# One body for two neighbouring time chunks: joint projections, norms and inverse, convolution taps from an SBUF copy, decay from rows of cumulative sums

## The chip, the cores and the metric

The kernel runs on one NeuronCore of one Trainium2 chip. The metric is the device time of one launch in microseconds (us). The engines are TensorE (PE in the profile, its weight loads PEld), VectorE (DVE), ScalarE (ACT), GpSimd (POOL) and SyncE, whose queue (SPq) issues the DMAs.

## The reference, cut to what matters

```python
# x (8, 1024, 128); 16 heads, key width 64, value width 128, 4 taps; then x + layernorm(attn(layernorm(x)))
q = l2(silu(conv4(x @ Wq.T)));  k = l2(silu(conv4(x @ Wk.T)));  v = silu(conv4(x @ Wv.T))
alpha = exp(-exp(A_log) * softplus(x @ Wa.T + dt_bias));  beta = 2 * sigmoid(x @ Wb.T)
def step(S, q_t, k_t, v_t, a_t, b_t):
    kS = k_t @ S
    S = a_t * (S - b_t * outer(k_t, kS)) + outer(k_t, v_t)
    return S, S.T @ q_t
o = rms_norm(o);  y = o @ Wo.T
# then x = x + layernorm(y), and a small feed-forward layer (token shift, three 128x128 products) with its own residual
```

All of it is float32.

## The kernel before

The recurrence is run in chunks of C = 64 tokens. A **step** is one chunk (of 16) of one pair of heads (of 8) for all 8 sequences: `STEPS` = 128 steps, in order, since the state `S` passes from chunk to chunk. The two heads of a pair lie on partitions 0 to 63 and 64 to 127. Most products are therefore 64x64 or 64x128, four of them side by side on the quadrants of the PE array; `CLASSES` are the sequences 0 to 3 and 4 to 7, which use different quadrants.

What a step does, by the names of its functions:

- `pe_proj` j = 0 to 3 (k, q, v of head 0, v of head 1): two matmuls of 4 x 67 columns each into PSUM banks 0 and 1. All four projections use these two banks. `act_tap0` multiplies the first tap out of PSUM into `cv`, `dve_conv` adds three more (L852), reading the projection from PSUM and `cv` from SBUF, 512 elements per partition each. Then a Silu.
- Norms: `pe_nk`, `pe_nq`, `pe_ms` sum squares over partitions with a moving operand of one column.
- Decay: `pool_lm` masks the log decay into `Lm` (two instructions, L967), `pe_dec` (L513) sums it up with triangular matrices, `act_exp` takes the exponential, `pool_dmn` and `pool_dmp` scale and mask it. The reset at the start of each pair of heads is a log decay of -1e4 (`RESET`).
- Products `pe_gram_k`, `pe_gram_p`, `pe_ktr`, `pe_ks`, `pe_vtr`; `dve_n` times `exN` gives `Nd`, `pool_nm` masks it to `NM`.
- The inverse of the 64x64 triangular matrix: the diagonal 16x16 blocks go through DRAM (`scrN`) into a layout with 64 blocks on 64 partitions, `pool_elim` (13 small instructions) and `dve_sub` (4 instructions of 512 elements) invert them, they go back through DRAM (`scrZ`, `scrX`), and two rounds of `pe_y`, `pe_z` with copies `act_y`, `act_x`, `dve_z0`, `act_z1` build the rest in `Z`.
- The recurrence: `pe_ks` (k times S), `dve_r`, `pe_u`, `act_u`, `pe_ds`, `pe_o`, `dve_s` (new S), `pool_sg` (S times decay); then `act_oc`, `act_osq`, `pe_ms`, `pe_wo` (L706), `act_yr` (8 scaled copies), `pool_acc` (L1016).

The work is software-pipelined by hand: one body holds the end of step l, the middle of l + 1 and the front of l + 2. The order on every engine is written out in `pe_body`, `act_body`, `dve_body`, `pool_body` and `sp_body`, and `program` runs three bodies before and three after a hardware loop of 124 bodies. Each engine does its list strictly in order, and the waits between them are on semaphores.

```python
with eng.Fori(1, STEPS - 3) as i:
    body(eng, i, i + 1, i + 2)
```

Of the kernel before, what the change touches and what calls it, by code (L numbers as in the profile page):

```python
# [18 lines left out]
P = 128  # L19
# [20 lines left out]
RESET = -1.0e4  # L40
# [6 lines left out]
K_N = K_XI + 272  # L47


def constants():  # L50

    c = np.zeros((P, K_N), np.float32)
    i = np.arange(P)
    same = (i[:, None] // C) == (i[None, :] // C)
    r, t = (i % C)[:, None], (i % C)[None, :]
    c[:, K_ID:K_ID + P] = np.eye(P)
    c[:, K_LE:K_LE + P] = same & (r <= t)
    c[:, K_GT:K_GT + P] = same & (r > t)
    c[:, K_BD:K_BD + P] = same
# [4 lines left out]
    c[:, K_XI:K_XI + 256:17] = 1.0  # L64
    return c


class Signal:
# [12 lines left out]
def build(nc, x, wtab, wo, wab, hcol, cst, wf, mu, out):  # L81
    with ExitStack() as ctx:
# [75 lines left out]
        bd_zero = sig("bd_zero")  # L158
# [23 lines left out]
        with nc.Block() as block:  # L182
# [13 lines left out]
            def _(pool):  # L196
# [18 lines left out]
            def _(dve):
# [64 lines left out]
            def _(act):  # L280
                act.wait_ge(zeroed.sem, 6)
# [67 lines left out]

        wkq_in = sig("wkq_in", 16)  # L350
# [15 lines left out]
        silu_q = sig("silu_q")
        silu_v = sig("silu_v", 2)
# [18 lines left out]
        x_in = sig("x_in", 64)  # L386
        v_tr = sig("v_tr")
        v_ok = sig("v_ok")
        k_tr = sig("k_tr")
        kt_ok = sig("kt_ok")  # L390
        pe_go = sig("pe_go")
        sp_go = sig("sp_go")
        y_mm = sig("y_mm", 2)
        y_ok = sig("y_ok", 2)
        z_mm = sig("z_mm", 2)
        z_ok = sig("z_ok", 2)
        x_mm = sig("x_mm")
        x_ok = sig("x_ok")
        ks_mm = sig("ks_mm")
        os_mm = sig("os_mm")  # L400
        o_mm = sig("o_mm")
        ds_mm = sig("ds_mm")
        sg_ok = sig("sg_ok", 2)
        n2_ok = sig("n2_ok")
        r2_ok = sig("r2_ok")
        rv_ln = sig("rv_ln")
        rv_ok = sig("rv_ok")
        bn_ok = sig("bn_ok")
        cr_ok = sig("cr_ok")
        nqs_ok = sig("nqs_ok")  # L410
        xi_ok = sig("xi_ok")
        xb_ok = sig("xb_ok")
        r0_ok = sig("r0_ok")
        r1_ok = sig("r1_ok")
        u0_mm = sig("u0_mm")
        u1_mm = sig("u1_mm")
        u0_ok = sig("u0_ok")
        u1_ok = sig("u1_ok")
        s0_ok = sig("s0_ok")
        s1_ok = sig("s1_ok")  # L420
        osq_ok = sig("osq_ok")
        oc_ok = sig("oc_ok")
        ms_mm = sig("ms_mm")
        ro_in = sig("ro_in")
        ro_ln = sig("ro_ln")
        ro_ok = sig("ro_ok")
        wo_mm = sig("wo_mm")
        yr_ok = sig("yr_ok")
        acc_ok = sig("acc_ok", 2)

        tabP3 = tabP[:].rearrange("p (n k) -> p n k", k=24)
        tabR3 = tabR[:].rearrange("p (n k) -> p n k", k=16)
        cv4 = cv[:].rearrange("p (i b t) -> p i b t", i=4, b=NB)
        v3 = lambda t, i: t[:, i * 512:(i + 1) * 512].rearrange("p (b t) -> p b t", b=NB)
        pj = bank(0, 2).rearrange("p (b t) -> p b t", b=NB)
        half = lambda t, g: t[:, g * 512:(g + 1) * 512]
        sq_kt, sq_qt = half(sq, 0), half(sq, 1)
        exN, exP = half(ex, 0), half(ex, 1)
        CLASSES = (range(0, 4), range(4, 8))
        r0r1, u_mms, u_oks, s_oks = (r0_ok, r1_ok), (u0_mm, u1_mm), (u0_ok, u1_ok), (s0_ok, s1_ok)  # L440
        osq = BD["KB"]
        yt = (half(BD["X"], 1), half(BD["Y"], 1))
        n2, r2, rv, bn, cr, nqs, ro = (sc[:, 8 * k:8 * k + 8] for k in range(7))
        row = lambda t: t.rearrange("p (o k) -> p o k", o=1)
        acc3 = accT[:].rearrange("p (c k) -> p c k", k=512)

        PB = {"dec": 4, "nk": 2, "gk": 2, "nq": 4, "gp": 2, "ktr": 4, "vtr": 4, "y0": 4, "z0": 4, "x": 2, "y1": 4, "z1": 6, "ks": 6, "u": 2, "o": 2, "ds": 6, "ms": 2, "wo": 6}
# [6 lines left out]
        def first(n):  # L454
            return isinstance(n, int) and n == 0
# [9 lines left out]
        def blk64(t, b, a):  # L465

            return t[a:a + 64, b * C:(b + 1) * C]
# [9 lines left out]
        def pair(bk, o=0):  # L477

            return bank(bk, 2).rearrange("p (g n) -> p g n", g=2)[:, :, o:o + 4 * C]

        def tiny(bk):

            return bank(bk, 2).rearrange("p (g n) -> p g n", g=2)[:, :, 0:4]
# [5 lines left out]
        def sv_out(h):  # L489

            a = sv[:].rearrange("p (b h t) -> p b h t", b=NB, h=2)[:, :, h, :]
            (ps_, pn), (bs, _), (ts, tn) = a.ap
            return bass.AP(a.tensor, a.offset, [(ps_, pn), (4 * bs + (1 - 2 * h) * C, 2), (bs, 4), (ts, tn)])


        def pe_proj(pe, n, j):
            w_in = (wkq_in, wv_in)[j // 2]
            pe.wait_ge(w_in.sem, w_in.at(n))
# [7 lines left out]
        def pe_dec(pe, n):  # L506
# [626 lines left out]
        def sp_body(sp, l, m, n):  # L1133
            if l is not None:
                sp_x_in(sp, l)
# [501 lines left out]
```

## Time and profile before

| | |
|---|---|
| time, median of 3 runs | 3735.81 us (3723.3, 3735.81, 3737.05) |
| span of the profiled execution | 3725.1 us |
| busy share: PE, PEld, DVE, ACT, POOL | 88%, 74%, 70%, 72%, 62% |
| matmul records | 77978 |
| mean granted TensorE clock | 0.922 of full speed |
| DMA, all queues | 226.12 MB, 61 GB/s over the span |

The profiled execution has its span as its own time; the median of the runs lies 10.7 us above it. Busy is the time in which an engine executes an instruction. The clock is given in parts of full speed, 2.4 GHz; it has two levels, 1.2 and 2.4 GHz.

### The profile page before, as it was taken

The numbers are of one execution on the slowest core, as the hardware profiler recorded it, in microseconds if no ns is written. First come the engines' busy times: TensorE is split into PE (matmuls) and PEld (weight loads), VectorE is DVE, ScalarE is ACT, GpSimd is POOL, SyncE is SP. The second block draws the span as 40 slices with busy tenths as digits, with TensorE's granted clock in tenths as the row PEclk, the third lists the DMA queues.
The fourth block names the chain that finished last, engine by engine and source line by source line (L and its number), as shares of the span: only waits on it lengthen the run. The fifth ranks groups of instructions, "written<-read, shape, count | busy, mean of one in ns | idle before, by whom it ended". The sixth has DMA issues, their size and how long they took to land. (4 is left out here: it accounts for less than half of the span.)

```text
span 3725.1 us, 195058 instructions
## 1 busy us (share of the span) xinstructions
PE 3292.6 (88%) x77978; PEld 2742.6 (74%) x77978; DVE 2605.8 (70%) x5465; ACT 2677.6 (72%) x5548; POOL 2301.4 (62%) x3558
## 2 busy tenths in 40 slices
PE   5699999999999999999999999999999999999775
PEld 4577777777777777777777777777777777777643
DVE  6677777777777777777777777777777777777453
ACT  2577777777777777777777777777777777777553
POOL 2456666666666666666666666666666666666345
PEclk9789999999999999999999999999999999999777
DMA  2223223232323232323323232323233232323111
GB/s 59 52 61 64 62 62 67 57 67 56 69 56 70 58 66 58 66 59 64 64 60 64 60 67 57 71 57 67 61 63 64 60 65 59 65 59 70 42 34 46
DMA packets 911057, 226.12 MB, mean 61 GB/s; under 512 B 820128, under 2 KB 894112, under 8 KB 911008
## 3 DMA queue, kind: packets, MB, share of 16 engines
q1 hardware_dynamic: 910848, 224.91, 28.8%
q8 instruction: 33, 0.54, 0.1%
q0 software_dynamic: 160, 0.53, 0.0%
q14 instruction: 16, 0.13, 0.0%
HBM read 169.73 MB, written 55.58 MB: 60 GB/s over the span
## 5 line engine op out<-in xcount | busy, mean ns | idle before, releaser
L852 DVE SCALAR_TENSOR_TENSOR cv<-ps,w_kq,cv 128x512 f32<-128x512 f32 x768 | 575.5, 749 | 417.1 <-ACT cv L719 403.5
L852 DVE SCALAR_TENSOR_TENSOR cv<-ps,w_v,cv 128x512 f32<-128x512 f32 x768 | 575.4, 749 | 153.0 <-ACT cv L719 134.9
L1016 POOL TENSOR_TENSOR accT<-accT,X 128x512 f32 (+1 forms) x128 | 163.3, 1276 | 530.2 <-ACT Y L817 530.2
L502 PE MATMUL ps<-xnT,w_kq 128*128 (+1 forms) x1024 | 325.7, 442 | 74.6 <-DVE cv L852 69.0
L502 PE MATMUL ps<-xnT,w_v 128*128 (+1 forms) x1024 | 335.2, 453 | 15.2 <-DVE cv L852 15.0
L1007 POOL TENSOR_TENSOR Sg<-S,tabR 128x512 f32<-128x512 f32 x256 | 333.8, 1323 | 0.0
L976 POOL TENSOR_TENSOR sc<-tabP,sc 128x8 f32<-128x8 f32 x128 | 26.3, 206 | 497.5 <-DVE sc L867 497.5
L765 ACT ACTIVATE Vt<-ps,sc 128x128 f32<-128x128 f32 x1024 | 278.8, 384 | 54.8 <-PE ps L571 54.8
L706 PE MATMUL ps<-wo_s,oo 128*128 128x128 f32 x2048 | 305.6, 309 | 1.2 <-issue 1.2
L967 POOL TENSOR_TENSOR Lm<-k_all,tabP 128x512 f32<-128x512 f32 x256 | 277.2, 1102 | 30.5 <-POOLq L182 30.5
L706 PEld LDWEIGHTS ps<-wo_s,oo 128*128 128x128 f32 x2048 | 280.8, 220 | 14.5 <-issue 1.7
L952 DVE SCALAR_TENSOR_TENSOR Rr<-ps,sc,Vt 128x128 f32<-128x128 f32 x1024 | 288.2, 344 | 1.3
L696 PEld LDWEIGHTS ps<-k_all,KB 128*128 128x128 f32 x2048 | 240.6, 193 | 58.7 <-issue 58.7
L637 PEld LDWEIGHTS ps<-Rr,Z 64*64 64x64 f32 x4096 | 238.1, 141 | 54.5 <-issue 54.5
L502 PEld LDWEIGHTS ps<-xnT,w_kq 128*128 128x128 f32 x1024 | 184.1, 200 | 126.0 <-issue 93.2
L637 PE MATMUL ps<-Rr,Z 64*64 64x128 f32 x4096 | 269.1, 284 | 1.9 <-issue 1.9
L696 PE MATMUL ps<-k_all,KB 128*128 128x1 f32 x2048 | 248.3, 251 | 5.9 <-ACT KB L802 2.1
L585 PEld LDWEIGHTS ps<-Z,NM 64*64 64x64 f32 x8192 | 187.4, 166 | 78.6 <-issue 78.6
L808 ACT ACTIVATE oo<-ps 128x1024 f32<-128x1024 f32 x128 | 131.2, 1025 | 154.3 <-PE ps L653 154.3
L585 PE MATMUL ps<-Z,NM 64*64 64x64 f32 x8192 | 213.2, 255 | 29.2 <-DVE Z L941 28.1
L653 PE MATMUL ps<-PT,U 64*64 64x64 f32 x8192 | 216.7, 221 | 23.8 <-PE ps L650 22.8
L719 ACT ACTIVATE cv<-ps,w_kq 128x512 f32<-128x512 f32 x256 | 174.3, 681 | 74.8 <-PE ps L502 74.7
(197 smaller groups left out, 8542.9 us busy)
## 6 DMA issues: line engine op xcount, KB each, us to landing
ex<-scrG SPq DMA_DIRECT2D x256, 128.0 KB, 2.9
scrN<-Nd SPq DMA_DIRECT2D x256, 128.0 KB, 2.6
Z<-scrZ SPq DMA_DIRECT2D x256, 128.0 KB, 3.2
X<-scrX SPq DMA_DIRECT2D x512, 64.0 KB
w_kq<-wtab SPq DMA_DIRECT2D x128, 132.0 KB, 2.2
w_v<-wtab SPq DMA_DIRECT2D x128, 132.0 KB, 2.5
wo_s<-wo SPq DMA_DIRECT2D x128, 128.0 KB, 2.8
NS<-scrN SPq DMA_DIRECT2D x128, 64.0 KB, 2.6
```

The lines of the kernel that those rows point to most:

```text
L502: last = nc.tensor.matmul(pj[:, 4 * g:4 * g + 4, 0:CW], w[:, (j % 2) * P:(j % 2 + 1) * P], xnT3[:, 4 * g:4 * g + 4, bass.ds((n % NC) * C, ...
L585: last = nc.tensor.matmul(ps[place(cls, a), col64(PB["y1" if l else "y0"], cls, i)], blk64(BD["NM"], b, a), blk64(BD["Z"], b, a), start=Tr ...
L637: last = nc.tensor.matmul(ps[a:z, col128(PB["u"], g, i)], blk64(BD["Z"], b, a), unit(Rr, b)[a:z], start=True, stop=True)
L653: last = nc.tensor.matmul(o_cols(h ^ cls, b, d), U[a:z, b * P + d:b * P + d + 64], blk64(BD["PT"], b, a), start=False, stop=(b == NB - 1))
L696: last = nc.tensor.matmul(ps[:, (PB["ms"] + h) * 512 + i:(PB["ms"] + h) * 512 + i + 1], osq[:, h * 512 + i * P:h * 512 + (i + 1) * P], kc( ...
L706: last = nc.tensor.matmul(ps[:, col128(PB["wo"], h, i)], oo[:, h * 512 + i * P:h * 512 + (i + 1) * P], wo_s[:, h * D:(h + 1) * D], start=T ...
L719: nc.scalar.activation(cv4[:, j], pj[:, :, 0:C], ACT.Copy, scale=tap(j, 0)).then_inc(tap0[j].sem, 1)
L765: last = nc.scalar.activation(unit(Vt, b), unit(ps, 4 * PB["vtr"] + b), ACT.Copy, scale=rv[:, b:b + 1])
L852: nc.vector.scalar_tensor_tensor(cv4[:, j], pj[:, :, k:k + C], tap(j, k), cv4[:, j], ALU.mult, ALU.add).then_inc(conv[j].sem, 1)
L952: last = nc.vector.scalar_tensor_tensor(unit(Rr, b), ps[:, col128(PB["ks"], g, i)], cr[:, b:b + 1], unit(Vt, b), ALU.mult, ALU.add)
L967: last = nc.gpsimd.tensor_tensor(v3(Lm, i), over(kc(o, C), NB, C), tabP3[:, bass.ds(n, 1), 0:8].rearrange("p o b -> p b o").to_broadcast([ ...
L1007: nc.gpsimd.tensor_tensor(half(Sg, g).rearrange("p (b v) -> p b v", b=4), half(S, g).rearrange("p (b v) -> p b v", b=4), gam, ALU.mult).th ...
```

## The change

Two neighbouring chunks of the same pair of heads, A and B (128 tokens), become one **pair**: `PAIRS` = 64 of them. A body now holds pair p0 (front), p1 (inverse and recurrence, first A, then B), p2 (rest of B, output) and p3 (last accumulations).

- Projections: one matmul of 512 columns for four sequences, without the 3 halo columns. `act_raw` copies the product from PSUM to `raw` in SBUF; `pool_tail` carries the last 3 columns over from the pair before. All four taps read `raw`: `act_tap0` and `dve_conv` now work on 1024 elements per partition with both inputs in SBUF.
- Norms: `nk`, `nq`, `ms` use 64 columns of ones in place of 1, on quadrants (`ms`: halves of columns); the small vectors hold both chunks.
- Decay: the cumulative sums are made once, in the prologue, and their rows stored in DRAM (`scrE`, and `scrG` their exponentials). Per pair, `sp_gr` broadcasts a row to 64 partitions, `pool_diff` subtracts the column, `act_abs` and `act_exp` give exp(-|difference|). `pool_lm`, `pe_dec` and `pool_nm` go. The reset is now zeros in the tables.
- Inverse: elimination and substitution run once per pair on 128 partitions. `Y` and `X` are single buffers for A and B in turn.
- `act_yr` (ScalarE) becomes `dve_yr` (VectorE, one instruction of 512 per half). `bn` and `cr` go from POOL to DVE. `sp_kc` copies B's keys to `kB` by DMA, so that `sk` is free for the next pair.
- The lists of all five engines are new. The loop has 58 bodies; 6 bodies stand before it and 4 after it.

```diff
-        def pe_proj(pe, n, j):
+        def pe_proj(pe, p, j):
...
             for g in range(2):
-                last = nc.tensor.matmul(pj[:, 4 * g:4 * g + 4, 0:CW], w[:, (j % 2) * P:(j % 2 + 1) * P],
-                                        xnT3[:, 4 * g:4 * g + 4, bass.ds((n % NC) * C, CW)], start=True, stop=True)
+                last = nc.tensor.matmul(bank(PB["P" + "kqvw"[j]] + g), w[:, (j % 2) * P:(j % 2 + 1) * P],
+                                        xnV[:, 4 * g:4 * g + 4, bass.ds((p % 8) * P, P)], start=True, stop=True)
...
+        def act_raw(act, p, j):
+            act.wait_ge(proj[j].sem, proj[j].at(p))
+            act.wait_ge(tail[j].sem, tail[j].at(p))
+            nc.scalar.activation(raw3[j][:, :, HALO:HALO + P], b3(bank(PB["P" + "kqvw"[j]], 2)), ACT.Copy).then_inc(raw_ok[j].sem, 1)
...
-                nc.vector.scalar_tensor_tensor(cv4[:, j], pj[:, :, k:k + C], tap(j, k), cv4[:, j],
-                                               ALU.mult, ALU.add).then_inc(conv[j].sem, 1)
+            nc.vector.scalar_tensor_tensor(cv3[j], raw3[j][:, :, k:k + P], tap(j, k), cv3[j],
+                                           ALU.mult, ALU.add).then_inc(conv[j].sem, 1)
...
+        def pe_ms(pe, p, s):
...
+            for i in range(4):
+                for h in range(2):
+                    for e, (c, d) in enumerate(HALF):
+                        o = h * 512 + (2 * i + e) * C
+                        last = nc.tensor.matmul(ps[c:d, col64(PB["ms"][s], h, i)], osq[:, o:o + C], kc(K_ONE, C), start=True, stop=True)
...
+        def act_abs(act, p):
+            act.wait_ge(diff_ok.sem, diff_ok.at(p))
+            nc.scalar.activation(E[:], E[:], ACT.Abs).then_inc(abs_ok.sem, 1)
...
+        def dve_yr(dve, p, s, h):
+            dve.wait_ge(wo_mm[h][s].sem, wo_mm[h][s].at(p))
+            dve.wait_ge(rt_ok.sem, rt_ok.at(p + 1))
...
+            nc.vector.tensor_tensor(half(yt, h).rearrange("p (i d) -> p i d", i=4),
+                                    bank(PB["wo"][s] + h).rearrange("p (i d) -> p i d", i=4), f, ALU.mult).then_inc(yr_ok[h][s].sem, 1)
...
+        def pool_tail(pool, p, j):
...
+            nc.gpsimd.tensor_tensor(raw3[j][:, :, 0:HALO], raw3[j][:, :, P:P + HALO],
+                                    tails[:, bass.ds(p, 1)].rearrange("p (o u) -> p o u", u=1).to_broadcast([P, NB, HALO]),
+                                    ALU.mult).then_inc(tail[j].sem, 1)
...
+        def sp_gr(sp, p):
+            if not first(p):
+                sp.wait_ge(pt_ok[B].sem, pt_ok[B].at(p - 1))
...
+                sp.dma_start(E[a:z], scrE[h, bass.ds(p, 1), :].to_broadcast([C, 1024])).then_inc(gr_in.sem, 16)
...
+            for i in range(6):
+                body(eng, *at(i))
+            with eng.Fori(2, PAIRS - 4) as j:
+                body(eng, j + 4, j + 3, j + 2, j + 1, j)
+            for i in range(PAIRS, PAIRS + 4):
+                body(eng, *at(i))
```

The new lists of the loop body, in order (0, 1, 2, 3 stand for the pairs p0 to p3):

```
PE:   proj 0k, 0q; ms 2B; ds 2B; ktr 1B; wo 2A; vtr 1A; proj 0v1; ks 1A; nq 1; y0 1A; proj 0v0; z0 1A; gk 0A; nk 0; x 1A; y1 1A;
      wo 2B (half); z1 1A; y0 1B; wo 2B (half); u 1A (half); z0 1B; u 1A (half); vtr 1B (half); y1 1B; vtr 1B (half); gk 0B; ds 1A;
      o1 1A; x 1B; ktr 0A; o2 1A; ks 1B; z1 1B; ms 1A; gp 0A; u 1B; o1 1B; gp 0B; o2 1B
DVE:  p 1B; sub 1 (4); ro_in 2B; conv 0k.1; s 2B; k 1B; yr 2A; conv 0k.2; cr 1; conv 0k.3, 0q.1; r 1A; nqs 1; r 1A; z0 1A; n2 0;
      conv 0q.2, 0q.3; yr 2B; r2 0; conv 0v0.1; bn 0; yr 2B; z0 1B; conv 0v0.2; n 0A, 0B; s 1A; k 0A; conv 0v0.3; r 1B; ro_in 1A;
      conv 0v1.1; p 0A; conv 0v1.2, 0v1.3
ACT:  raw 0k; tap0 0k; raw 0q; xb 1; table; ln 1; tap0 0q; root 1; oc 2B; v 1A; raw 0v1; table; silu_k 0; y0 1A; sq_k 0; raw 0v0;
      tap0 0v0; x 1A; y1 1A; abs 0; z1 1A; y0 1B; table; exp 0; u 1A; y1 1B; v 1B; table; silu_q 0; x 1B; osq 1A; z1 1B; tap0 0v1;
      u 1B; oc 1A; silu_v0 0; osq 1B; silu_v1 0
POOL: tail 0k; sg 2B; xi 1; sq_q 1; elim 1 (13); acc 3B; tail 0v0, 0q; acc 3B; sg 2B; tail 0v1; acc 2A; sg 1A; diff 0; qg 1; acc 2A;
      sg 1A; eb 0A, 0B; ep 0
SP:   wkq 0; gram 1A, 1B; gram_in 1; kc 1; xr 1; gr 0; wo 2; wv 0; z_out 1; x_out 1; z_in 1; x_in 1A, 1B
```

## Rows read from the trace of the kernel before

**Rows 1.** The page's busy times: busy us, share of the span, instructions.

```profile
PE 3292.6 (88%) x77978; PEld 2742.6 (74%) x77978; DVE 2605.8 (70%) x5465; ACT 2677.6 (72%) x5548; POOL 2301.4 (62%) x3558
```

**Rows 2.** Windows: from:to, length, busy us of PE, PEld, DVE, ACT, POOL, clock, DMA share.

```profile
1000.00:1500.00 500.00, 458.52 (x11400) 386.54 (x11400) 363.48 (x704) 380.65 (x799) 326.40 (x514) 0.94 0.30 62
...
1546.00:1547.00 1.00, 1.00 (x30) 0.88 (x23) 0.72 (x2) 1.00 (x1) 1.00 (x2) 0.50 0.45 101
```

**Rows 3.** Timeline of PE: start, length, line, tiles, count, [idle before it and releaser].

```profile
1502.53 1.17 PE L502 MATMUL ps<-xnT,w_kq 128*128 x4 [0.50 <-DVE cv L852]
...
1528.93 1.17 PE L502 MATMUL ps<-xnT,w_kq 128*128 x4 [0.50 <-DVE cv L852]
1530.03 1.96 PE L637 MATMUL ps<-Rr,Z 64*64 64x128 f32 x32
...
1537.36 0.69 PE L564 MATMUL ps<-k_all,sl 64*64 64x64 f32 x32
...
1539.83 1.07 PE L513 MATMUL ps<-Lm,k_all 64*64 64x256 f32 x16
1540.94 1.92 PE L696 MATMUL ps<-k_all,KB 128*128 128x1 f32 x16
1543.21 0.64 PE L523 MATMUL ps<-k_all,sq 64*64 64x1 f32 x32 [0.35 <-DVE sc L881]
...
1553.11 1.06 PE L533 MATMUL ps<-k_all,sq 64*128 64x1 f32 x16 [0.33 <-ACT Y L780]
```

**Rows 4.** Groups by form, 1000 to 2000 us: busy us, mean ns, idle before.

```profile
L852 DVE SCALAR_TENSOR_TENSOR cv<-ps,w_kq,cv 128x512 f32<-128x512 f32 x228 | 170.9, 750 | 122.1 <-ACT cv L719 118.1
...
L967 POOL TENSOR_TENSOR Lm<-k_all,tabP 128x512 f32<-128x512 f32 x76 | 83.8, 1123 | 0.0
...
L1260 ACT ACT_TABLE_LOAD x38 | 48.8, 1283 | 0.7
...
L960 DVE TENSOR_TENSOR S<-ps,Sg 128x512 f32<-128x512 f32 x76 | 48.7, 682 | 6.7 <-PE ps L653 4.6 <-POOL Sg L1007 1.8
...
L1022 POOL TENSOR_TENSOR NM<-Nd,k_all 128x512 f32<-128x512 f32 x38 | 48.4, 1273 | 0.0
...
L817 ACT ACTIVATE Y<-ps,sc 128x128 f32<-128x128 f32 x148 | 42.9, 397 | 0.0
...
L928 DVE TENSOR_TENSOR tmpS<-XT,tmpW 64x512 f32<-64x512 f32 x38 | 40.6, 1068 | 1.3
...
L808 ACT ACTIVATE oo<-ps 128x1024 f32<-128x1024 f32 x38 | 38.9, 1025 | 43.6 <-PE ps L653 43.6
...
L921 DVE TENSOR_TENSOR tmpS<-NS,XT 64x512 f32<-64x512 f32 x38 | 33.2, 874 | 0.0
```

**Rows 5.** Groups by form with 1024 elements: a vector sum, a ScalarE pass.

```profile
L256 DVE TENSOR_TENSOR U<-U,S 128x1024 f32<-128x1024 f32 x1 | 1.2, 1226 | 4.0 <-ACT Rr L301 4.0
...
L1553 ACT ACTIVATE U<-U 128x1024 f32<-128x1024 f32 x8 | 8.5, 1057 | 0.3
```

**Rows 6.** Instructions of one line: ns min/median/max, whole span, then 1000 to 2000 us.

```profile
L921 DVE TENSOR_TENSOR tmpS<-NS,XT x128: 673/828/5560, 124.7 to 3481.0; 64x512 f32<-64x512 f32 x128
...
L1007 POOL TENSOR_TENSOR Sg<-S,tabR x76: 1031/1482/1772, 1005.8 to 1983.0; 128x512 f32<-128x512 f32 x76
```

**Rows 7.** Timeline of DVE in the first bodies.

```profile
124.74 3.59 DVE L921 TENSOR_TENSOR tmpS<-NS,XT 64x512 f32<-64x512 f32 x1
```

**Rows 8.** Timeline of POOL in the same stretch.

```profile
123.52 2.04 POOL L967 TENSOR_TENSOR Lm<-k_all,tabP 128x512 f32<-128x512 f32 x2
125.53 1.26 POOL L1029 TENSOR_TENSOR QG<-sl,ex 128x512 f32<-128x512 f32 x1
126.75 1.03 POOL L990 TENSOR_TENSOR sq<-sl 128x512 f32<-128x512 f32 x1
```

**Rows 9.** Timeline of PE behind the loop's end.

```profile
3457.50 0.46 PE L653 MATMUL ps<-PT,U 64*64 64x64 f32 x15 [0.93 <-issue]
...
3469.88 3.35 PE L706 MATMUL ps<-wo_s,oo 128*128 128x128 f32 x14 [0.89 <-issue]
```

More of the change, by code:

```diff
@@ new lines, in pe_ms, with pe_wo @@
+            last.then_inc(ms_mm[s].sem, 1)
+        def pe_wo(pe, p, s, h):
+            pe.wait_ge(wo_in.sem, wo_in.at(p))
+            pe.wait_ge(oc_ok[s].sem, oc_ok[s].at(p))
+            pe.sem_inc(pe_go.sem, 1)
+            for i in range(4):
+                last = nc.tensor.matmul(ps[:, col128(PB["wo"][s], h, i)], oo[:, h * 512 + i * P:h * 512 + (i + 1) * P],
+                                        wo_s[:, h * D:(h + 1) * D], start=True, stop=True)
+            last.then_inc(wo_mm[h][s].sem, 1)
@@ new lines, in act_ln, with act_ln_out @@
+        def act_ln(act, p):
+            act.wait_ge(n2_ok.sem, n2_ok.at(p))
+            if not first(p):
+                act.wait_ge(ro_in[B].sem, ro_in[B].at(p - 1))
+            act_ln_out(act, p)
+            nc.scalar.activation(sc[:, 32:64], sc[:, 0:32], ACT.Ln).then_inc(ln_ok.sem, 1)
+        def act_ln_out(act, p):
+            if not first(p):
+                for g in range(2):
+                    act.wait_ge(v_ok[g][B].sem, v_ok[g][B].at(p - 1))
+                if not (isinstance(p, int) and p == 1):
+                    for h in range(2):
+                        act.wait_ge(yr_ok[h][B].sem, yr_ok[h][B].at(p - 2))
@@ new lines, in act_v @@
+        def act_v(act, p, s, h):
+            act.wait_ge(v_tr[h][s].sem, v_tr[h][s].at(p))
+            act.wait_ge(rt_ok.sem, rt_ok.at(p))
+            if s == B:
+                act.wait_ge(u_mm[h][A].sem, u_mm[h][A].at(p))
+            elif not first(p):
+                act.wait_ge(u_mm[h][B].sem, u_mm[h][B].at(p - 1))
+            for i in range(4):
+                b = 4 * h + i
+                last = nc.scalar.activation(unit(R, b), ps[:, col128(PB["vt"][s], h, i)], ACT.Copy, scale=rv[:, 8 * s + b:8 * s + b + 1])
+            last.then_inc(v_ok[h][s].sem, 1)
@@ new lines, in sp_wv, with sp_wo @@
+        def sp_wv(sp, p):
+            if not first(p):
+                sp.wait_ge(conv[3].sem, conv[3].at(p - 1))
+                sp.wait_ge(conv[2].sem, conv[2].at(p - 1))
+            sp.sem_inc(sp_go.sem, 1)
+            sp.dma_start(w_v[:].rearrange("p (o k) -> p o k", o=1), wtab[:, bass.ds(p // 8, 1), 1, :]).then_inc(wv_in.sem, 16)
+        def sp_wo(sp, p):
+            if not first(p):
+                for h in range(2):
+                    sp.wait_ge(wo_mm[h][B].sem, wo_mm[h][B].at(p - 1))
@@ new lines, in sp_kc, with sp_gram @@
+        def sp_kc(sp, p):
+            sp.wait_ge(silu[0].sem, silu[0].at(p))
+            if not first(p):
+                sp.wait_ge(ks_mm[B].sem, ks_mm[B].at(p - 1))
+            sp.dma_start(kB[:], half(sk, B)).then_inc(kc_in.sem, 16)
+        def sp_gram(sp, p, s):
+            sp.wait_ge(nd_ok[s].sem, nd_ok[s].at(p))
+            if not first(p):
+                sp.wait_ge(n_in.sem, n_in.at(p - 1))
+            for h, (a, z) in enumerate(HALF):
+                sp.dma_start(rows(scrN, h)[:, 8 * s:8 * s + 8], b3(half(Nd, s)[a:z])).then_inc(n_out.sem, 16)
@@ L1352, in build, with at @@
+        def program(eng, body):
+            def at(i):
+                return [i - s if 0 <= i - s < PAIRS else None for s in range(5)]
+            for i in range(6):
[4 more added lines that the diff above has]
+                body(eng, *at(i))
         with nc.Block() as block:
```

1862 lines of the change are left out of this document (1070 added, 792 removed).

## Prediction

> **What bounds the kernel now.** The page's first part [rows 1] says PE is busy 88% of the span and every other engine 62% to 74%. Averages over unlike stages say little, so next the windows: from 240 to 3400 us the kernel repeats one body, and a stretch of 500 us there [rows 2] has PE at 458.5 us, 92%, DVE at 73%, ACT at 76%, POOL at 65%, DMA at 30%. Then the timeline of PE: the k projection starts at 1502.53 and again at 1528.93 [rows 3], so a step takes 26.40 us, 128 steps 3379 us, and 3725.1 - 3379.2 = 345.9 us lie around them (prologue, filling and draining, feed-forward). The reader is to see that PE waits only for 0.3 to 0.5 us at a time (four of some seven times in a body are in the rows): 26.4 x 0.92 = 24.2 us busy, 2.2 us idle. The granted clock has a second toll. It is 0.94 on average and falls to 1.2 GHz once a body, as at 1546 us [rows 2], after a stretch of products with one column and a wait (`ms`, `nk` [rows 3]). At 0.94, some 12% or 3.2 us of a body run at half speed, which forgoes 1.6 us of full-clock work at most; a part of it falls into waits, so I take 1.4. So a step is 22.8 us of PE work at full clock, 1.4 us for the slow stretch, 2.2 us of waits; two steps, a pair, are 45.6 + 2.8 + 4.4 = 52.8 us. What the change is worth is the length of the new body, P, against 52.8.
>
> **PE's work.** `dec` goes: it starts at 1539.83 and `ms` follows at 1540.94, 1.11 us, twice: -2.2. The projections: 1528.93 to 1530.03 is 1.10 us for 2 matmuls of 268 columns in 4 records. At 2.4 GHz and two cycles per float32 column, 268 columns take 0.223 us a record, 0.89 for the four; the other 0.21 is the loading of weights. 512 columns take 0.427 a record, so a call is 4 x 0.427 + 0.21 = 1.92 us (all in proportion to columns, it would be 2.1). Four calls per pair instead of eight: 7.7 for 8.8, -1.1. `nq`: today 16 records over 128 weight columns, 1.06 [rows 3], 0.99 from start to start, twice; new 64 records on quadrants. A group of 32 such records takes 0.62 from start to start whether it has 64 columns (0.69 long) or one (0.64 long) [rows 3], so 1.24 for 1.98, -0.7; `nk` likewise stays as it is. `ms` has 1.92 us for 16 records with 128 weight columns [rows 3]; new 32 records with half the weight columns and 64 moving ones. Bounds: half of today's or, if each record costs what one costs now, double; I take the same 1.92, since half the weights twice over are the same load. That leaves -1.9 to +3.8 per pair. All else only changes place: 1216 records per pair for 1200. Sum 45.6 - 4.0 = 41.6 us.
>
> **VectorE's.** Today 363.5 us in 18.94 bodies is 19.2 us, 38.4 per pair [rows 2]. A tap from PSUM takes 0.750 for 512 elements [rows 4]. From SBUF with 1024 there is none; a plain sum of that size takes 1.226 [rows 5], and the tap's form costs 0.07 more than a sum (0.750 against 0.682 [rows 4]): 1.29. Bounds 1.23 and 2 x 0.75. Twelve for twenty-four: 15.5 for 18.0, -2.5. The substitution (874 + 1068 ns and two reductions [rows 4]) is done once, not twice: -3.3. `dve_yr` adds 4 x 0.69 = 2.8, `bn` and `cr` 0.4, fewer small ones -0.5. Sum 35.3.
>
> **ScalarE's.** Today 380.65 / 18.94 x 2 = 40.2 per pair. It loses the scaled copies of `yr` (L817, two such groups of 1.13 a step [rows 4], 4.5 per pair), a second `xb` and small ones (1.4), and the taps and Silus become passes of 1.06 [rows 5] for two of 0.63 to 0.70 (-2.3). It gains four `raw` copies of 1.025 [rows 4] and `act_abs`, 1.06; `exp` halves (-1.0). Four table loads of 1.283 [rows 4] remain. About 36 to 37. **POOL's**: 326.4 / 18.94 x 2 = 34.5; minus `lm` 4.5 and `nm` 2.5 [rows 4], one elimination 3.5, `bn`/`cr` 0.8, plus `diff` 2.0, tails 1.0: 26 to 27. **SP and DMA**: 32 issues of 0.3 to 0.65 us per pair become 25. Nothing waits long in front: `xr` waits for `os` of B, `gr` behind it for `pt` of B, and `wo`, `wv` queue behind both; each lands some 3 us later, while PE needs `wo` 7 us into the body. DMA at 30% has room for the 0.4 MB more. These cost nothing unless the issue order slips by more than 2 us.
>
> **The order.** I walked one new body with these durations, PE's k projection at 0. On PE `ks` A ends at 13, `z0` A 17.5, `nk` 19.4, `z1` A 22, `u` A 26, `gk` B 28.7, `o1` A 31, `ks` B 34, `u` B 39, `o2` B 42. On DVE `conv` k is done at 11.4, `r` A 15.7, then it waits 1.8 for `z0` and 0.9 for `nk`; `n` B 29.5, S after A 32.8, `r` B 37.0, last tap 41.7. ACT ends near 44 but starts as late. PE hardly waits, so P = 42 without disturbance; but from 31 us on DVE has no idle left, and PE waits for its `r` B and `p` A. What DVE loses there is lost.
>
> **The port.** Today DVE has two instructions per step with both inputs in SBUF (L921, L928). L921 takes 673 ns at best and 874 on average; POOL's L1007 beside it 1031 at best, 1482 in the median [rows 4, 6]. At 124.74 L921 takes 3.59 us, until POOL's four instructions from 123.52 on have ended, 0.55 us behind them [rows 7, 8]. So the two engines do not run such work side by side. Per step L921 and L928 (1.7 us) add 0.26 to DVE and about 1.2 (L1007 0.55, L1016 0.5, L967 0.15) to POOL, 85% of their length. The change makes all taps such instructions: 15.5 + 1.7 = 17.2 us per pair. In the walk nine of twelve taps meet POOL at work: 9 x 1.29 + 1.7 = 13.3 us, 85% is 11.3, half of it (5.6) on DVE; today's split gives it 2, a POOL that always wins far more. Of 5.6 some 1.6 fall into DVE's waits: +4. The Trainium skill, "SBUF — State Buffer", SBUF: two separate sides, says that a VectorE instruction with two SBUF inputs and a GpSimd instruction that reads SBUF exclude each other for the whole instruction. The rows agree. By that rule alone 17.2 + 24.5 us of undisturbed POOL work need the port one after the other, 41.7 us, just the PE's floor.
>
> **The sum.** 41.6 for PE, half of the 2.8 for the slow clock (the one-column groups go, the waits do not): 1.4; port 4: P = 47.0. Around the loop: filling and draining is now one front body (28 us), one without a front (35) and one tail (12) beyond 63 whole ones, 28 us over 64 P where today has 51: -23. Straight-line code costs: behind the loop PE stops 0.93 us with no one to wait for, 249 matmul records further 0.89 [rows 9]; such stops are absent in the loop. Some 4900 more records stand outside the loop now, 20 stops, +18; prologue +3. So 345.9 stays, give or take 20. 345.9 + 64 x 47.0 = 3353.9, on the scale of the median + 10.7 = 3365 us, 10% less.
>
> **Rivals.**
> (a) PE keeps today's waits and slow stretches, 7.2 us a pair, because every group has new waits on PSUM banks: P = 48.8, 3480 us. For it: the body has 88 waits on PE. Against: the projections no longer hold banks 0 and 1 through three taps.
> (b) All is hidden: P = 43.3, 3128 us. Against it: DVE without idle at the body's end.
> (c) Slower: POOL wins the port. If at each of the nine taps DVE waits 2.0 us (at 124.74 it was 2.9), DVE has 35.3 + 18 + 4 of other waits = 57.3: 4024 us. It turns slower from (52.8 - 39.3) / 9 = 1.5 us per tap. Against: in the loop L921 waits 0.2 on average.
> (d) The loop's PE code, twice as long, no longer stays resident: five stops of 0.93 in each body: P = 51.6, 3659 us. No row tells what fits; 600 records do. The Trainium skill, "Runtime: NRT & Kernel Launch", Instruction fetch mechanics, gives PE room for 2048 instructions and says that a branch to code outside the window must fetch; by it some 1300 fit.
> (e) No change: savings and new waits cancel, P = 52.8, 3736 us.
>
> **Chances.** Forecast (P 45 to 49.5, but for a) 0.43, (a) 0.22, (b) 0.10, (d) 0.06, (c) 0.15, (e) 0.04. A measurement can tell 0.5% from no change. Faster 0.81, same 0.04, slower 0.15. The range takes in (a), (d) and part of the way to (b), and leaves out (c) and the full (b): 3200 to 3690 (P 44.4 to 52.0; `ms` at its bounds moves P by -1.9 or +3.8 and stays inside).
>
> **What would show it.** The distance of two k projections on PE is P. PE: no L513 group, projections of 1.9 us, `ms` of 1.9. The clock above 0.94. DVE taps: 1.29 alone, in the mean 1.5 to 1.8 if the port costs as said, above 2.8 for (c). No instruction packets inside the loop, else (d). Wrong it would be if DVE waits long for PE or ACT in the middle of the body (then the order, not the work, sets P), or if `ms` costs double.

## The result and the profile after

The changed kernel takes 4168.18 us (median of 4 runs, 4153.61 to 4169.99), the one before 3736.43: a ratio of 1.116, 95% interval 1.114 to 1.119. It is slower by 11.6% where the forecast was 10% faster. All profiles here lie within 0.7% of their medians.

The page of the changed kernel: busy times, and from its list of queues the one that brings code.

```profile
PE 3091.5 (74%) x79010; PEld 2392.8 (57%) x79010; DVE 2762.5 (66%) x4634; ACT 2475.7 (59%) x3772; POOL 2154.9 (52%) x2143
...
q8 instruction: 761, 12.47, 1.4%
```

Beside [rows 1] no engine is fuller: PE went from 88% to 74%, DVE from 70% to 66%. Nothing has become the bound by its work. What is new is q8, the queue that brings instructions: 761 packets of code, where the kernel before has 33 in all and none between 240 and 3400 us. A stretch in the loop, as in [rows 2], then a short one:

```profile
1000.00:1500.00 500.00, 377.02 (x9896) 290.17 (x9894) 336.31 (x492) 300.04 (x461) 266.60 (x261) 0.86 0.33 63
...
1538.00:1547.00 9.00, 7.02 (x8) 2.36 (x8) 0.32 (x1) 2.18 (x2) 2.24 (x3) 0.50 0.51 96
```

The granted clock is 0.86 for 0.94. A clock of either 1 or 0.5 that averages 0.86 is at half speed 28% of the time. PE's timeline, as in [rows 3], shows where the loop jumps back:

```profile
1532.28 0.65 PE L543 MATMUL ps<-sl_q,sk 64*64 64x64 f32 x32
1532.75 0.65 PE L646 MATMUL ps<-PT,U 64*64 64x64 f32 x32
1538.14 2.92 PE L500 MATMUL ps<-xnT,w_kq 128*128 x3 [4.74 <-issue]
1542.91 4.58 PE L500 MATMUL ps<-xnT,w_kq 128*128 x5 [1.84 <-issue]
1547.41 1.15 PE L696 MATMUL ps<-k_all,osq 128*64 128x64 f32 x32
```

L646 is the body's last work, L500 the next one's first, the k projection. PE stands 4.74 us with no one to wait for, sends three product records, stands 1.84 us more, and meanwhile the clock has fallen: from 1538 to 1547 it is 0.50 (1.2 GHz). Eight product records that need 3.8 us at full clock (the v projections, 1.88 for four at 1552.75) take 9.3. There is a second slow stretch in this body:

```profile
1503.00:1509.00 6.00, 5.16 (x133) 4.92 (x134) 3.61 (x7) 1.58 (x3) 0.00 (x0) 0.50 0.02 5
```

It comes behind a stop of 1.59 us (at L603) and a wait of 2.05 for DVE (at L533); the two stretches, 6.5 and 10.5 us, are the 28%. The same groups over the trace from 1000 to 2000 us (count | busy, mean ns | idle before, releaser):

```profile
L500 PE MATMUL ps<-xnT,w_kq 128*128 x128 | 119.3, 1087 | 97.2 <-issue 97.2
...
L646 PE MATMUL ps<-PT,U 64*64 64x64 f32 x2048 | 64.7, 222 | 52.1 <-issue 52.1
...
L533 PE MATMUL ps<-sk 64*64 64x64 f32 x1056 | 23.9, 229 | 35.0 <-DVE sc L911 35.0
```

All groups' idle time that ends on "issue" sums to 204.3 us in these 1000. P, the time of one pair in the loop, from 43 starts of one DVE instruction (L904) between 515.5 and 3077.6 us, is 2562.1 / 42 = 61.0 us, so that is 12.5 us a pair; before it was 0. The only long wait for another engine is PE's for DVE at L533, 2.1 us a pair. The kernel before, by 99 starts of L1029, has 26.31 us a step, 52.6 a pair.

VectorE's taps (L872), which were L852 in [rows 4]:

```profile
L872 DVE SCALAR_TENSOR_TENSOR cv<-raw,w_kq,cv 128x1024 f32<-128x1024 f32 x101 | 207.8, 2071 | 0.6
...
L872 DVE SCALAR_TENSOR_TENSOR cv<-raw,w_v,cv 128x1024 f32<-128x1024 f32 x97 | 143.0, 1475 | 3.6 <-ACT cv L720 1.0
```

2.07 and 1.48 us, in the mean 1.77. The 1.29 that was forecast for a tap alone is the median of the k and q taps over the whole span (ns min/median/max):

```profile
L872 DVE SCALAR_TENSOR_TENSOR cv<-raw,w_kq,cv x384: 1271/1286/3428, 108.4 to 3880.9; 128x1024 f32<-128x1024 f32 x192
```

Where P stands for a run, it comes from its one profiled execution. The medians of all its executions can differ by up to 23 us, 0.4 us a pair.

### The profile page after: what moved, and what is told of

It is laid out like the page before. It is cut to its first block and busy times, and to the rows that moved or that the text cites. A ratio compares the mean times of both kernels' runs of the same rounds, so it can differ in the third digit from the quotient of the medians.

```text
span 4168.0 us, 187403 instructions
## 1 busy us (share of the span) xinstructions
PE 3091.5 (74%) x79010; PEld 2392.8 (57%) x79010; DVE 2762.5 (66%) x4634; ACT 2475.7 (59%) x3772; POOL 2154.9 (52%) x2143
## 5 line engine op out<-in xcount | busy, mean ns | idle before, releaser
L1088 POOL TENSOR_TENSOR accT<-accT,yt 128x512 f32 (+1 forms) x256 | 405.0, 1582 | 756.5 <-DVE yt L1001 743.2
L872 DVE SCALAR_TENSOR_TENSOR cv<-raw,w_kq,cv 128x1024 f32<-128x1024 f32 x384 | 778.8, 2041 | 19.6 <-ACT cv L720 17.2
L500 PE MATMUL ps<-xnT,w_kq 128*128 (+1 forms) x512 | 441.9, 1015 | 355.0 <-issue 347.9
L712 ACT ACTIVATE raw<-ps 128x1024 f32<-128x1024 f32 x256 | 265.6, 1038 | 532.8 <-PE ps L500 531.3
L872 DVE SCALAR_TENSOR_TENSOR cv<-raw,w_v,cv 128x1024 f32<-128x1024 f32 x384 | 565.4, 1472 | 13.6 <-ACT cv L720 4.0
L500 PEld LDWEIGHTS ps<-xnT,w_kq 128*128 128x128 f32 x512 | 142.3, 301 | 579.2 <-issue 578.0
L646 PE MATMUL ps<-PT,U 64*64 64x64 f32 x8192 | 257.0, 222 | 186.4 <-issue 186.0
L982 DVE SCALAR_TENSOR_TENSOR R<-ps,sc,R 128x128 f32<-128x128 f32 x1024 | 280.4, 338 | 77.3 <-PE ps L622 75.5
L704 PE MATMUL ps<-wo_s,oo 128*128 128x128 f32 x2048 | 317.4, 310 | 6.8 <-issue 3.9
L646 PEld LDWEIGHTS ps<-PT,U 64*64 64x64 f32 x8192 | 213.7, 136 | 184.6 <-issue 184.6
L704 PEld LDWEIGHTS ps<-wo_s,oo 128*128 128x128 f32 x2048 | 279.8, 216 | 22.8 <-issue 7.6
L802 ACT ACTIVATE R<-ps,sc 128x128 f32<-128x128 f32 x1024 | 278.8, 385 | 0.1
L633 PE MATMUL ps<-R,Z 64*64 64x128 f32 x4096 | 265.1, 271 | 1.8 <-issue 1.3
L576 PE MATMUL ps<-Z,Nd 64*64 64x64 f32 x8192 | 223.0, 243 | 50.1 <-issue 38.1
L500 PE MATMUL ps<-xnT,w_v 128*128 (+1 forms) x512 | 253.0, 616 | 9.2 <-DVE KT L937 6.3
L576 PEld LDWEIGHTS ps<-Z,Nd 64*64 64x64 f32 x8192 | 190.6, 154 | 74.5 <-issue 69.5
```

The costliest lines, as they stand in the source:

```text
L500: last = nc.tensor.matmul(bank(PB["P" + "kqvw"[j]] + g), w[:, (j % 2) * P:(j % 2 + 1) * P], xnV[:, 4 * g:4 * g + 4, bass.ds((p % 8) * P, P ...
L576: last = nc.tensor.matmul(ps[place(cls, a), col64(PB["y1" if l else "y0"][s], cls, i)], blk(Nd, s, b, a), blk(Z, s, b, a), start=True, sto ...
L633: last = nc.tensor.matmul(ps[a:z, col128(PB["u"][s], g, i)], blk(Z, s, b, a), unit(R, b)[a:z], start=True, stop=True)
L646: last = nc.tensor.matmul(ps[d:d + 64, o:o + C], U[a:z, b * P + d:b * P + d + 64], blk(PT, s, b, a), start=False, stop=(b == NB - 1))
L704: last = nc.tensor.matmul(ps[:, col128(PB["wo"][s], h, i)], oo[:, h * 512 + i * P:h * 512 + (i + 1) * P], wo_s[:, h * D:(h + 1) * D], star ...
L712: nc.scalar.activation(raw3[j][:, :, HALO:HALO + P], b3(bank(PB["P" + "kqvw"[j]], 2)), ACT.Copy).then_inc(raw_ok[j].sem, 1)
```

## The experiments

Two theories. **Code**: PE's loop no longer stays in the engine (it is not *resident*), so it is fetched anew in every turn, and PE stands still for it, mostly at the jump. **Port** (or the new waits): taps and POOL block each other, and PE's stops are a by-product. To count code I count PE's instructions in the loop: the page has as many PEld as PE records (x79010 both), so a product comes with its own weight load, and a float32 call makes two of each. With the few other instructions, the loop before has about 1245, the new one 2513. Runs with one execution (the `b_` kernels and `a_hint_np`, `a_line_np`) have no interval of their own.

**1. Only the code of the kernel before made longer: `b_x2`.**

```diff
-            with eng.Fori(1, STEPS - 3) as i:
-                body(eng, i, i + 1, i + 2)
+            per = 2 if eng.engine == mybir.EngineType.PE else 1
+            with eng.Fori(1, STEPS - 3, per) as i:
+                for k in range(per):
+                    body(eng, *(i + (k + s) for s in range(3)))
```

> The kernel before, with PE's loop written as 62 turns of two steps each instead of 124 turns of one; the other engines' code and all work unchanged. Counted in instructions of PE's program (a float32 product is two weight loads and two products), PE's loop body goes from about 1245 to 2489; the changed kernel's is 2513. Theory (code no longer stays resident): code packets appear all through the loop, PE shows stops with no one to wait for near each start of the doubled body and at some places in it, the granted clock falls, and two steps take 52.8 us plus 8 to 12: 4150 to 4500 us. Rival (port, waits or PSUM banks of the new body are what costs): this kernel has none of them, so it stays within 1% of 3736 us.

Measured: 4491.5 us beside 3724.8. The first row is the code queue, the others PE's groups from 1000 to 2000 us:

```profile
q8 instruction: 770, 12.62, 1.2%
...
L502 PE MATMUL ps<-xnT,w_kq 128*128 x244 | 94.7, 522 | 75.6 <-issue 72.2 <-DVE cv L852 3.3
...
L706 PE MATMUL ps<-wo_s,oo 128*128 128x128 f32 x496 | 82.4, 334 | 19.9 <-issue 19.9
```

Same work, same taps from PSUM, and two steps take 65.1 us for 52.6 (80 starts of L1029). 12.5 us are lost by nothing but a loop of 2489 instructions: there are stops of 9.1 us a turn where there were none and 4.5 us more of busy time at a clock of 0.87 for 0.94, and PE waits 1.1 less for others. The longest, 4.7 us a turn, is at the k projection, where the changed kernel has 5.9. That settles that code alone can do it.

**2. How long may the loop be: `b_pad3`, `b_pad6`, `b_pad11`, `b_pad14`.** In the kernel before (`b_pad3` as shown; 7, 12 and 15 in place of 4 for the others):

```diff
 def pe_nk(pe, n):
...
-            for i in range(4):
+            for i in list(range(4)) * 4:
```

> The kernel before with 3 more repetitions of pe_nk's products: 1438 instructions in PE's loop. With 11 repetitions (1950 instructions) all code was fetched anew in each turn and a step took 48.3 us, 15.6 more than its work. Theory (the whole loop and the code fetched ahead of its end must fit in about 2048, so the bound lies between 1300 and 1600): either no code packets in the loop and 1.7 us of work a step more, 3920 to 3950 us, or, if the bound is below 1438, ten packets less two a turn and 5000 us or more.

> The kernel before with 6 more repetitions of pe_nk's products: 1630 instructions in PE's loop. With 1438 no code packet appeared in the loop, with 1950 all of it was fetched in each turn. Resident: 3.4 us of work a step more, with the clock's share 4.2 to 4.6: 4260 to 4320 us and no packets. Not resident: some 8 to 9 packets a turn and 5300 us or more.

> The kernel before, with the 16 products of pe_nk repeated 11 more times into the same place, so that the result is the same; PE's loop body has some 1950 instructions. Each repetition costs about 0.57 us of PE time, 6.3 us a step if PE bounds it, 4450 to 4550 us. Theory (room for some 2048 instructions): no code packets inside the loop. Rival (there is no such bound, or the bound is lower): as many code packets per instruction as the next kernel, or none in either.

> As the kernel with 11 repetitions, but 14: some 2140 instructions in PE's loop body. By work alone 1.7 us a step more than with 11, 210 us in all. Theory (room for some 2048): code packets in every turn of the loop, and stops of PE with no one to wait for, 5 us or more a step beyond the 1.7: over 800 us more than with 11. Rival: 210 us more and no packets.

```
kernel    instructions  us       a step   over before  code packets in the loop
before    1245          3725     26.3                  none
b_pad3    1438          4014     28.5      2.2         none
b_pad6    1630          4299     30.8      4.5         none
b_pad11   1950          6360     47.2     20.9         10 a turn
b_pad14   2142          6237     46.2     19.8         10 a turn
```

Up to 1630 instructions each repetition costs 0.72 to 0.75 us, work and a somewhat lower clock (0.91, 0.89). That is more than I expected for `b_pad3` (4014 us for 3920 to 3950), and its theory, a bound between 1300 and 1600, is refuted by `b_pad6`, which was within its range. (The 48.3 us a step that the expectation gives for `b_pad11` are 47.2 by the starts of L1029.) Between 1630 and 1950 the loop falls out: by 0.75 a repetition 8.2 of the 20.9 us are work, 12.7 a step are not, 8.2 of these being stops. The code queues of the pages of `b_pad6` and `b_pad11`:

```profile
q8 instruction: 41, 0.67, 0.1%
```

```profile
q8 instruction: 1277, 20.92, 1.4%
```

My expectation of a bound between 1950 and 2142 was wrong, and so was that of more time with 14 repetitions than with 11; with 14 the stops sum to 5.7 us a turn for 8.2 with 11, mainly because those ahead of L653 (1.4 us) and L523 are gone or shorter; why they are is open. The Trainium skill, "Runtime: NRT & Kernel Launch", Instruction fetch mechanics, gives PE room for 2048 instructions in blocks of 256, and the next block is fetched while one runs. The packets fit that: written out (experiment 4) a body of 2513 takes 193 packets in 19.7 bodies, 9.8 each, 256 instructions a packet; the body before, written out (experiment 5), takes 172 in 35.5 steps, 4.85 each, which is 1241. The changed kernel takes 196 in 16.4 bodies, 12.0 each: some two more. That these are fetched past the jump and thrown away, and that such blocks are why 1950 doesn't fit in 2048, is argued, not shown.

**3. The jump announced: `a_hint`.**

```diff
-            with eng.Fori(2, PAIRS - 4) as j:
+            with nc.Fori(2, PAIRS - 4, engines=[eng.engine],
+                         hint_back_edge=eng.engine == mybir.EngineType.PE) as j:
```

> The changed kernel, whose PE loop carries a hint that its last branch will be taken. The body is 2513 instructions as before. Theory: part of the loss is the stop at the jump back (4.8 us, with 9.5 us of slow clock behind it); if the hint makes the code for the start of the body come early, that stop goes and the pair is 4 to 8 us shorter, 3650 to 3900 us. The stops inside the body stay, for its code has to be brought in every turn. If the hint has no effect, 4168 us. Rival (port and waits cost, not code): 4168 us either way.

Measured: 3776.4 us, ratio to before 1.012 (1.009 to 1.015); P = 54.5 (48 starts of L904). One argument of the loop gives 392 us back, where the port's theory had nothing, so a good part of the loss is at the jump. The two packets are gone too: 183 in 1000 us, 10.0 a body. The code queue from 1000 to 2000 us, in the changed kernel and in `a_hint`, then PE's groups in `a_hint`:

```profile
q8 instruction: 196, 3.21, 1.5%
```

```profile
q8 instruction: 183, 3.00, 1.3%
```

```profile
L500 PE MATMUL ps<-xnT,w_kq 128*128 x144 | 96.2, 829 | 56.2 <-issue 56.2
...
L646 PE MATMUL ps<-PT,U 64*64 64x64 f32 x2336 | 71.4, 221 | 41.7 <-issue 41.6
```

The stop ahead of L500 is 3.1 us a pair for 5.9, all stops 165.8 us or 9.0 a pair, the clock 0.92 for 0.86.

**4. No jump, or half as many: `a_line`, `a_hint_x2`.**

```diff
-            with eng.Fori(2, PAIRS - 4) as j:
-                body(eng, j + 4, j + 3, j + 2, j + 1, j)
+            if eng.engine == mybir.EngineType.PE:
+                for j in range(2, PAIRS - 4):
+                    body(eng, j + 4, j + 3, j + 2, j + 1, j)
+            else:
+                with eng.Fori(2, PAIRS - 4) as j:
+                    body(eng, j + 4, j + 3, j + 2, j + 1, j)
```

> The changed kernel with PE's loop written out, 58 bodies one behind the other, no jump. If the first code after a jump is what costs, a pair loses all 5.8 us of it: P = 48, 3410 to 3480 us, faster than the kernel before. The stops inside a body (about 0.8 to 2.2 us each, some five in a body) stay. Rival (the port or DVE's chain bounds the pair once PE is freed): P = 52 to 53, 3680 to 3740 us.

> The changed kernel with the hint at PE's jump back and two bodies per turn of PE's loop (29 turns, 5018 instructions each); other engines unchanged. Every instruction of PE's loop is fetched in any case; what changes is that the jump comes half as often. With the hint alone a pair takes 53.8 us, and around the jump PE loses 2.84 us ahead of the k projection and about 3 us more inside the 8 projection products behind it. Theory (the first code after a jump comes late): half of 5.8 us per pair goes, 2.5 to 3 us, 64 pairs: 3580 to 3630 us. Rival (these stops are not the jump's, PE merely catches up with the fetch wherever its code is dense; or the port bounds the pair): 3740 to 3780 us.

(`a_hint_x2` has two bodies in each turn of PE's loop, with the hint.) `a_line`: 3617.1 us, ratio 0.971 (0.968 to 0.974): faster than the kernel before. P = 50.9 (51 starts), the clock 0.96. Both ranges that I had given missed: it lies between the theory's 3410 to 3480 us and the rival's 3680 to 3740. Every instruction is still fetched, once; what is gone is the jump, and with it the stop ahead of L500. The stops that are left, 118.0 us in 1000 or 6.0 a pair, are spread over a dozen groups; the three with the most, and L576:

```profile
L704 PE MATMUL ps<-wo_s,oo 128*128 128x128 f32 x624 | 88.5, 291 | 21.7 <-issue 21.0 <-DMA wo_s<-wo 0.7
...
L646 PE MATMUL ps<-PT,U 64*64 64x64 f32 x2496 | 72.0, 220 | 17.9 <-issue 17.9
...
L643 PE MATMUL ps<-QG,S 64*64 64x64 f32 x2496 | 69.1, 221 | 16.0 <-issue 15.2
...
L576 PE MATMUL ps<-Z,Nd 64*64 64x64 f32 x2560 | 63.2, 234 | 42.7 <-DMA Z<-scrZ 35.3 <-issue 7.2
```

The last row is what PE waits for most in this kernel: the DMA that brings the inverse's blocks back into `Z`, 1.8 us a pair. In the jump form it is 0.4 us in 1000.

`a_hint_x2`: 3792.1 us, 1.018 (1.015 to 1.021), P = 54.3: no gain over the hint alone. Its stop at L500 did halve (27.5 us in 1000 for 56.2), but those at L643 and L704 grew from 14.2 and 0 to 23.1 and 18.1, and all sum to 151.2 for 165.8. The clock is 0.90 for 0.92. So my reading that half the jumps save half of their cost is wrong; why no jump at all saves 3.6 us more (by the medians of the runs 2.5) is open.

**5. Written out, the kernel before: `b_line`.** The same edit in the kernel before.

> The kernel before with PE's loop written out, so that every instruction is fetched once, where the loop's stay in place today. Theory (fetching itself costs where PE's code is dense, in the written-out changed kernel 6 us of stops per 2513 instructions): per step of 1245 instructions 3 us of stops, less what falls into waits, 2 to 3 us: 3980 to 4130 us. If fetching in a straight line costs nothing and only jumps do: 3725 us, within 1%.

Measured: 3955.3 us, 28.2 us a step (93 starts of L1029), 1.9 more than in place. Fetching costs without any jump, 3.7 us for two steps of together 2490 instructions. The expectation, 3980 to 4130 us, was a little high. The stops are 1.3 us a step, PE is busy 0.8 longer (the clock is 0.93 for 0.94), and its waits for other engines are a little less.

**6. The port: `a_hint_np`, `a_line_np`.**

```diff
-            nc.gpsimd.tensor_tensor(sq[:], sl_q[:], sl_q[:], ALU.mult)
+            nc.gpsimd.tensor_tensor(sq[:, 0:64], sl_q[:, 0:64], sl_q[:, 0:64], ALU.mult)
...
-            nc.gpsimd.tensor_tensor(QG[:], sl_q[:], QG[:], ALU.mult)
+            nc.gpsimd.tensor_tensor(QG[:, 0:64], sl_q[:, 0:64], QG[:, 0:64], ALU.mult)
...
-            nc.gpsimd.tensor_tensor(dst, dst, row(half(yt, h)), ALU.add)
+            nc.gpsimd.tensor_tensor(dst[:, :, 0:64], dst[:, :, 0:64], row(half(yt, h))[:, :, 0:64], ALU.add)
```

These two kernels leave out a part of the computation.

> The changed kernel with the hint, and with POOL's pass over the squares of q (1.89 us), its product for QG (3.34 us) and its four sums into acc (1.6 us each) cut to a sixteenth or an eighth of their columns; it leaves out that part of the computation. About 10.5 us of POOL's two-input work per pair go, the q and k taps (2.05 us in the mean, 1.29 alone) fall to 1.4 to 1.6. If the port costs the pair time: P = 53.8 less 2 to 4 us, 3520 to 3660 us. If fetching alone bounds it: 3776 us, within 1%.

> The changed kernel with PE's loop written out and POOL's passes for the squares of q, for QG and for acc cut to a sixteenth or an eighth of their columns; that part of the computation is left out. The same cut took the jump form from 3776 to 3665 us, 1.7 us a pair, and emptied PE's waits for DVE. If port and fetch add up: 3617 less 1.3 to 1.9 us a pair, 3495 to 3535 us. If the fetch's stops only spread into the room that is made: 3580 us or more.

With the hint 3665.2 us (just above the range of the expectation) and P = 52.2 for 54.5; written out 3474.3 (below its range) and P = 48.8 for 50.9. PE's wait for DVE at L533, first in `a_line`, then in `a_line_np`:

```profile
L533 PE MATMUL ps<-sk 64*64 64x64 f32 x1280 | 29.0, 230 | 26.4 <-DVE sc L911 26.4
```

```profile
L533 PE MATMUL ps<-sk 64*64 64x64 f32 x1280 | 27.6, 223 | 0.0
```

The k and q taps fall from 2.05 to 1.57 us and from 2.09 to 1.53. The cut gives 2.3 and 2.1 us a pair (by the medians 1.7 and 2.2), whether code is late much or little. It does not come off PE's waits alone: in the written-out form L533's 1.3 us and 0.6 us of waits for DMA go, PE is busy 1.0 us less (the clock is 0.98 for 0.96), and the stops for code grow from 6.0 to 7.2. That the port is what costs these 2 us is argued: the cut also shortens POOL's own chains, and no run holds those apart. How it happens, from DVE's and then POOL's timeline of `a_hint`:

```profile
1541.27 6.29 DVE L872 SCALAR_TENSOR_TENSOR cv<-raw,w_kq,cv 128x1024 f32<-128x1024 f32 x2
1547.48 1.11 DVE L982 SCALAR_TENSOR_TENSOR R<-ps,sc,R 128x128 f32<-128x128 f32 x4
1548.52 0.16 DVE L911 TENSOR_SCALAR sc<-ps 128x16 f32<-128x16 f32 x1
```

```profile
1541.28 1.90 POOL L1016 TENSOR_TENSOR E<-E,tabP 128x1024 f32<-128x1024 f32 x1
1543.14 3.34 POOL L1042 TENSOR_TENSOR QG<-sl_q,QG 128x1024 f32<-128x1024 f32 x1
1546.44 2.24 POOL L1088 TENSOR_TENSOR accT<-accT,yt 128x512 f32 x1
```

Two taps of 1.29 take 6.29 us. L1016 has its usual 1.90, and L1037, a POOL pass over as many elements, takes 1.89; so the four one after the other would be an estimated 6.4 us. They end 6.3 us after the first start, about when they would one after the other. L1042 loses some 1.4 us by it and the taps 3.7. L911, for which PE's L533 waits, is queued behind them.

**7. Squares of q on ScalarE: `a_line_sq`.**

```diff
                 act_osq(act, p1, B)
             if p0 is not None:
+                act_sq_q(act, p0)       # activation(sq, sl_q, Square), after nk
                 act_silu_v(act, p0, 1)
...
-                pool_sq_q(pool, p1)
+                pass
```

PE's loop is written out as in `a_line`.

> The changed kernel with PE's loop written out, and the squares of q made by ACT (a pass of 1.06 us at the end of its body) in place of POOL (1.89 us, both inputs in SBUF, beside the q taps). If the port still costs the pair time in this form: the q and k taps fall below 2 us and the pair gets 0.5 to 1.5 us shorter, 3520 to 3590 us beside 3617 of the written-out kernel. If not: 3617 within 0.5%; if ACT's 1.06 us now come late for PE, up to 3680.

Measured: 3656.5 us, 0.983 (0.979 to 0.987), P = 52.1: worse than `a_line` by 1.2 us a pair (by the medians 0.6). The k and q taps stayed at 2.07 us, so they do not lose their time to this pass of POOL; PE's wait for L911 (here L916) grew from 26.4 to 34.8 us in 1000, and a wait for ACT of 6.4 us came up:

```profile
L533 PE MATMUL ps<-sk 64*64 64x64 f32 x1216 | 31.8, 253 | 34.8 <-DVE sc L916 34.8
...
L603 PE MATMUL ps<-XY,X 64*64 64x64 f32 x1216 | 30.6, 227 | 13.2 <-issue 6.8 <-ACT XY L818 6.4
```

POOL's 1.89 us were not what counted. That ACT's 1.06 came late is read from these waits; they are 0.8 of the 1.2 us.

## Why the prediction was wrong

**The step that failed** is rival (d): "The loop's PE code, twice as long, no longer stays resident", with a chance of 0.06 and "five stops of 0.93 in each body". It was the case, and the prediction's own sign for it, instruction packets inside the loop, is what the page shows. The forecast itself put this term at nothing: its sum has stops only around the loop, because "such stops are absent in the loop", which holds for the kernel before and was carried over to a body of twice the code. Two things in (d) were wrong.

*The count.* I took the 1216 records of PE's products in a pair against room for "some 1300", worked out from the 2048 instructions that the Trainium skill, "Runtime: NRT & Kernel Launch", Instruction fetch mechanics, gives. But [rows 1] has PEld x77978 beside PE x77978: each product record has a load record of its own. 1216 records are 2432 instructions, 2513 with waits and the rest, and the 600 that "do fit" are 1245. With that count the 2048 of the Trainium skill speak for (d), not against it. By the runs what fits is less still, 1630 but not 1950.

*The price.* [rows 9] gave 0.93 us for a stop in straight-line code, and I put that on five. Such stops exist (`b_line`: 1.3 us of them a step). The jump is another thing: 4.74 us, 1.84 behind it, and 9 us at the low clock. With the other stops of the body that is 12.5 us of stops a pair, and the clock goes from 0.94 to 0.86. (d) as priced gave P = 51.6; the row was of the wrong kind of place.

**The other terms.** *PE's work*, 41.6 us at full clock: `a_line_np` has the clock at 0.98 to 0.99 and 824.7 us busy in 1000, at P = 48.8 that is 40.3. Right, a little high: `ms` takes 1.15 us a step, not 1.92, so it is near the lower bound of half; the projections take 1.88 to 1.98 for 1.92. *VectorE* without the port, 35.3: there 770.7 us busy in 1000, 37.6 a pair, with part of the port still in it. *ScalarE*, 36 to 37: 601.0 x 0.0610 = 36.7. *POOL*, 26 to 27: 528.1 x 0.0610 = 32.2; it loses time to the taps as well (L1042 takes 3.34 us), but that this is the whole difference is not shown. *The port*: taps of 1.5 to 1.8 in the mean was right (1.77), the 4 us of P looks about twice too high (2.1 to 2.3 for a large part of POOL's passes, and not all of that need be the port). Rival (c) did not happen: POOL does not always win, both lose. *The clock*: "above 0.94" failed in the loop with the jump and came true without it (0.96). *DMA*, "These cost nothing": so it is in the jump form, but written out PE waits 1.8 us a pair for `Z`. *Around the loop*, 345.9: 4168.0 - 64 x 61.0 = 264 us, which is 82 us less. The bodies outside the loop, six pairs' worth, pay no jump; by the 10.1 us below that is an estimated 60 us. Written out it is 3592.5 - 64 x 50.9 = 335, so the term was nearly right.

**The account of P**: 61.0 in the changed kernel; 50.9 without the jump, so the jump costs 10.1: 6.5 as stops (12.5 for 6.0), 4.7 as busy time at the lower clock (46.0 for 41.3), 0.8 more of PE's waits for DVE, and 1.8 less of those for DMA. Then 48.8 with a part of POOL's passes gone. In 48.8 there are still 146.5 us of stops in 1000, 7.2 us a pair. Fetching without jumps costs 3.7 us for as many instructions in the kernel before; taken off 50.9 it would leave 47.1, beside the forecast's 47.0. That is an estimate: no version of this body stays resident, so none showed it. By that estimate the change does save what it was said to save, some 5 us a pair (52.6 to 47.1), and pays 14 for its code. That the forecast's 47.0 is so close is in part luck: it held 4 us for the port, and nothing for the wait for `Z`.

## What to carry to other kernels

Count the instructions of a loop per engine, weight loads included (PE and PEld records of one turn), before merging or unrolling bodies; here 1630 stayed in PE and 1950 did not, and going over cost 12.7 us a turn. Whether code is fetched is one row of the page (q8) and "issue" in front of PE's groups; look there first when every engine got emptier. If a body can't be made shorter, do without the jump on that engine or announce it: written out, this change is 2.9% faster than the kernel before it instead of 11.6% slower.

## What the runs showed of the hardware

- The hint at the jump back was worth 6.5 us a turn, and with it the packets of code went from 12.0 to 10.0 a turn.
- A stop of 4.74 us was followed by 9 us at 1.2 GHz (1538 to 1547 us), though PE had work in them for 7.0 us: what a stop costs is more than its length.
- Straight-line code is not free either: 1.9 us a step of 1245 instructions (`b_line`).
- A loop of 2142 instructions was shorter in time than one of 1950 with less work (46.2 and 47.2 us a turn). Its stops are 2.5 us shorter; why stays unexplained.
- `ms` with 64 weight columns takes 1.15 us for 32 product records; with 128 weight columns and one moving column it took 1.92 for 16 [rows 3].
